# A fused attention and feed-forward layer: the softmax probabilities turned by VectorE blocks and a trip through device memory instead of by TensorE

## The chip, the cores and the metric

One core of a Trainium2 chip runs the whole layer in one launch. The metric is the device time of one execution in microseconds, lower is better. Three runs of the kernel before took 946.12, 946.64 and 946.98 us, median 946.64.

## The reference

A residual stream `x` of 2 batches of 1024 tokens and 512 features passes a gated linear attention, then a feed-forward block, then a softmax attention, then the same feed-forward block again. The part that the change touches is the softmax attention (full, no causal mask, scores over all 1024 tokens of a batch):

```python
scale = 1.0 / jnp.sqrt(jnp.asarray(x.shape[-1], x.dtype))
Q = jnp.einsum('bsd,de->bse', x, W_q)
K = jnp.einsum('bsd,de->bse', x, W_k)
```

then softmax of the scaled Q K^T over the keys, times V, times W_o, added to the stream. The kernel folds W_q with W_k, and W_v with W_o, ahead of time.

## The kernel before, in words

Each engine has an instruction queue of its own, written out by hand; an engine runs its queue strictly in order and waits on semaphores. The stages follow one another: "A" (linear attention, batches 0 and 1), "mid" (weights), "F1" (feed-forward, two blocks), "B" (softmax attention, batches 0 and 1, about 468 to 723 us of the span), "F2" (feed-forward, two blocks). Products are made in f16 or f32r as a high part and a low part, three matmuls for each product (high by high, low by high, high by low).

Stage B, for each batch `b`: tokens are in 8 tiles (rows) of 128. `query` makes the left operands, four for each half of the batch. `values(i)` makes the value tile i. The scores of a pair of rows (rows 2p and 2p+1) come from seven sub-products ("pieces" 1 to 7, a Strassen-like scheme), each six matmuls in one PSUM bank: pieces 1, 6, 7, 4 pass one after the other through bank 4, and pieces 2, 5, 3 through bank 5. ScalarE copies bank 4 to `probs` (`part_sum`), VectorE adds bank 5 to it (`part_add`). Then for row i: VectorE `row_max(i)`, ScalarE `softmax(i)` (exp in place in `probs[i % 2]`, 128 x 1024 f32), TensorE `turn_probs(i)` (eight 128x128 transposes into two PSUM banks), ScalarE `pT_high(i)` (high f16 part of the turned tile), VectorE `pT_low(i)` (low part), TensorE `attend(i)` (24 matmuls), VectorE `out_add(i)` (divide by the row sum, add to the stream).

Between these, the next block's input is normalised and turned (sets B1 or F2): VectorE `x_stats`, `x_normalise`, `x_second`, `x_34_low`; TensorE `turn_both`; ScalarE `x_copy`, `x_row_highs`, `x_12_high`, `x_34_high`; GpSimd `x_sums` and the low parts. `query_parts` on VectorE and GpSimd, with `a_copy`, `a_highs`, `s_high` on ScalarE, split the queries.

There is no planner: the order of work is the order of the calls in each engine's queue. In the stages before and after B, three of the six input sets (F1, B0, F3) are already turned without TensorE: `x_blocks` (VectorE, 32x32 blocks in place), `blocks_to_dram` and `blocks_to_turned` (the SP queue, four transfers out and four back for a 128 x 1024 tile).

```python
def turn_probs(i):
    use = turn_use(b, i)
    pe.wait_ge(probs_done, b * 8 + (i + 1))
    u.free(use)
    ...
    for t in range(BT):
        last = nc.tensor.transpose(bank(use[0], 2)[:, t * P:(t + 1) * P],
                                   probs[i % 2][:, t * P:(t + 1) * P], ident[:, :])
    last.then_inc(filled[use[0]], 1)
```

Of the kernel before, what the change touches and what calls it, by code (L numbers as in the profile page):

```python
# [5 lines left out]
F32 = mybir.dt.float32  # L6
# [39 lines left out]

X_STATS = {(0, 2): ((0,), (1,), (2, 3)), (0, 3): ((4,), (5,), (6, 7))}
# [24 lines left out]
def ffn_uses(**more):  # L72
    uses = {0: 24, 1: 20, 2: 13, 3: 12, 4: 10, 5: 2, 6: 2, 7: 2}
    for name, n in more.items():
# [10 lines left out]
          ("B", 0, {0: 13, 1: 13, 2: 8, 4: 16, 5: 12, 6: 5, 7: 5}),  # L85
          ("B", 1, {0: 10, 1: 10, 2: 7, 4: 17, 5: 12, 6: 4, 7: 4}),
# [28 lines left out]
def hybrid_layer_kernel(nc, x, wq, wk, wv, w_ab, bq, bk, bv, b_ab,  # L115
# [3 lines left out]
    def at(name, offset, cols, dtype=F32):  # L119
# [18 lines left out]
           for v in range(2)]  # L138
# [76 lines left out]
               (Z + 112896, Z + 114944, Z + 116992), (Z + 86016, Z + 88064, Z + 90112))  # L215
# [57 lines left out]
    turned_lo = [at(f"turned_lo{b}", (Z + 47104, Z + 8192)[b], BTOK, F16) for b in range(2)]  # L273

# [5 lines left out]
    blocks = nc.dram_tensor("blocks", [4 * len(MOVED), QUADS, 2 * KT, P, SQ], F32, kind="Internal").ap()  # L280

# [117 lines left out]
    row_a_done = sem("row_a_done")  # L399
    row_b_done = sem("row_b_done")  # L400
# [179 lines left out]
    def pT(b, i):  # L580

        if i < 3:
            return tuple(t[b][:, :].rearrange("p (g n) -> p g n", g=2) for t in (turned_hi, turned_lo))
        if (b, i) in ((1, BT - 1), (1, BT - 2)):
            c = BTOK * (BT - 1 - i)
            return tuple(t[:, c:c + BTOK].rearrange("p (g n) -> p g n", g=2) for t in (s_hi, s_lo))
        return tuple(t[b][:, :].rearrange("p (k n) -> p k n", k=KT)[:, 0:2, GROUP:BTOK] for t in (xb_hi, xb_lo))
# [58 lines left out]
    def score_use(piece, p):  # L646
        return {1: (4, 4 * p), 6: (4, 4 * p + 1), 7: (4, 4 * p + 2), 4: (4, 4 * p + 3),
                2: (5, 3 * p), 5: (5, 3 * p + 1), 3: (5, 3 * p + 2)}[piece]

    def turn_use(b, i):  # L650
        return (4, 16) if (b, i) == (1, BT - 1) else (2, i)
# [24 lines left out]
    with block as blk:  # L676

        @blk.sync
        def _(sp):
# [126 lines left out]

            weights_out()
            for q in MOVED:
# [6 lines left out]
                if q == B0:  # L815
                    weights_back()
            store(0, *range(BT))
# [6 lines left out]
        def _(pool):  # L824
# [221 lines left out]

            query_parts(0, 0)
# [3 lines left out]
            query_parts(1, 0)  # L1051
            x_rstd(F2, *range(8))
            pool.wait_ge(x_34_lo, 4 * B1 + 4)
            for dst, src, less in ((3, 7, 1), (4, 2, 0), (5, 3, 1)):
                nc.gpsimd.tensor_tensor(cols(w_s, dst, HID), cols(w_gu, src, HID), cols(w_s, less, HID),
                                        ALU.subtract).then_inc(ws_ready, 1)
            query_parts(1, 1)
            pairs_of(F2)
            ffn("F2", 0)
# [4 lines left out]
        def _(act):  # L1064
# [335 lines left out]
            for b in range(BATCHES):  # L1400
# [6 lines left out]
                def part_sum(piece, p):  # L1407
# [3 lines left out]
                    row, half = {1: (0, 0), 6: (0, 1), 7: (1, 1), 4: (1, 0)}[piece]  # L1411
                    nc.scalar.activation(cols(probs[row], half), bank(4), ACT.Copy).then_inc(drained[4], 1)  # L1412
# [7 lines left out]
                def pT_high(i):  # L1420
                    use = turn_use(b, i)
                    u.full(use)
                    nc.scalar.activation(pT(b, i)[0], bank(use[0], 2).rearrange("p (g n) -> p g n", g=2), ACT.Copy,  # L1423
                                         scale=PS).then_inc(pT_hi_done, 1)

# [9 lines left out]
                for i in range(1, 6):  # L1435
                    v_high(i)
                part_sum(1, 0)
                part_sum(6, 0)
                part_sum(7, 0)
                v_high(6)  # L1440
                part_sum(4, 0)
                softmax(0)
                v_high(7)
                for p in range(4):
                    if (b, p) == (1, 3):
                        softmax(7)
                    pT_high(2 * p)
                    if p == 1:
                        a_copy(b, 1, 0)
                    elif p < 3:  # L1450
                        part_sum(1, p + 1)
                    if (b, p) != (1, 3):
                        softmax(2 * p + 1)
                    if p == 1:
                        a_copy(b, 1, 1)
                        a_highs(b, 1, 0)
                        s_high(b, 1, 0)
                        a_highs(b, 1, 1)
                        s_high(b, 1, 1)
                    if p == 2:  # L1460
                        x_34_high(B1 if b == 0 else F2, 1)
                    if p == 3 and b == 0:
                        x_34_high(B1, 3)
                        a_copy(1, 0, 0)
                        a_copy(1, 0, 1)
                    if p == 3 and b == 1:
                        x_copy(F2, 3)
                        x_highs(F2, 3)
                    pT_high(2 * p + 1)
                    if p == 1:  # L1470
                        part_sum(1, 2)
                    if p < 3:
                        part_sum(6, p + 1)
                        part_sum(7, p + 1)
                    q = B1 if b == 0 else F2
                    if p in (1, 2):
                        x_copy(q, 2 * p - 2)
                        x_highs(q, 2 * p - 2)
                    if p == 2 and b == 0:
                        x_copy(q, 3)  # L1480
                        x_row_highs(q, 3)
                    if p < 3:
# [1258 lines left out]
```

## Time and profile before

| what | value |
|---|---|
| median of three runs | 946.64 us |
| the profiled execution's own time | 945.55 us |
| its span in the profile | 943.8 us |
| TensorE busy | 930.4 us, 99% |
| VectorE, ScalarE, GpSimd busy | 608.2, 445.3, 425.9 us (64%, 47%, 45%) |
| matmul clock granted | full in all 40 slices |
| DMA in stage B | close to idle |

Engines are named PE (TensorE matmul), PEld (its weight loads), DVE (VectorE), ACT (ScalarE), POOL (GpSimd), SPq (the SP engine's DMA queue). L numbers are lines of the kernel. Matmul ends are modelled, so the start-to-start distance is the cost of a matmul on the engine.

### The profile page before, as it was taken

The page shows a single profiled execution, that of the slowest core. Times are in us where ns is not written, and L with a number is a line of the kernel's source. Part 1 is how long each engine was busy: PE and PEld are TensorE (multiplying, and loading weights), DVE is VectorE, ACT ScalarE, POOL GpSimd, SP SyncE. Part 2 cuts the span into 40 slices and gives each one's busy share as a digit, 9 for nine tenths or more (in the row PEclk, how much of TensorE's full clock was granted, in tenths as well). Part 3 has the DMA queues.
Part 4 walks back from the last instruction along what each step waited for, and adds up shares of the span by engine and source line. Part 5 has one row for each costly group of instructions (what it writes and reads, how often), then busy time and mean ns, then how long its engine had stood idle before and what let it go on. Part 6 is the DMA issues. An engine that isn't in the chain of part 4 may idle for free.

```text
span 943.8 us, 13107 instructions
## 1 busy us (share of the span) xinstructions
PE 930.4 (99%) x4654; PEld 525.6 (56%) x4670; DVE 608.2 (64%) x1148; ACT 445.3 (47%) x884; POOL 425.9 (45%) x447
## 2 busy tenths in 40 slices
PE   7999999999999999999999999999999999999998
PEld 4888988888734444444444455444455444444444
DVE  7555656949777777767655466446466777766643
ACT  4443334356577634663333354323455686246620
POOL 5433424377357654665630043304333466545530
PEclk9999999999999999999999999999999999999999
DMA  9501300024211190015500000000000001910001
GB/s 314 181 11 34 134 23 23 1 91 135 68 66 45 23 157 1 1 23 81 107 14 1 1 1 1 1 1 1 1 1 1 1 1 23 186 59 1 1 34 56
DMA packets 115008, 44.97 MB, mean 48 GB/s; under 512 B 101952, under 2 KB 102272, under 8 KB 114688
## 3 DMA queue, kind: packets, MB, share of 16 engines
q1 hardware_dynamic: 114944, 44.13, 18.1%
q8 instruction: 38, 0.62, 0.3%
q14 instruction: 26, 0.21, 0.1%
HBM read 32.56 MB, written 11.57 MB: 47 GB/s over the span
## 4 chain that ended last, share of the span: by engine, by line
PE 93%; DVE 2%; ACT 1%; POOL 1%; DMA 1%; SPq 1%; issue 1%; DVEq 0%; POOLq 0%
PE psum L2211 54%; PE psum L2458 14%; PE psum L2460 13%; PE psum L2608 7%; PE psum L2619 1%; DMA bq_col<-bq 1%; PE psum L2260 1%; PE psum L2345 1%; PE psum L2249 1%; ACT probs L1417 0%; DVE xb_lo L2116 0%; ACT xb_hi L1423 0%; DVE ln_bn L1532 0%; POOL wvT_lo L1007 0%; SPq L686 0%
## 5 line engine op out<-in xcount | busy, mean ns | idle before, releaser
L972 POOL TENSOR_TENSOR hid<-hid,hid_hi 128x512 f32<-128x512 f32 x88 | 102.9, 1170 | 110.1 <-DVE hid_hi L1888 110.1
L2458 PE MATMUL psum<-xf,w_gu 128*128 128x512 f16 x352 | 133.8, 380 | 0.1
L2458 PE MATMUL psum<-xf,w_s 128*128 128x512 f16 x264 | 100.1, 379 | 1.5 <-DVE up L1861 1.3
L2460 PE MATMUL psum<-xf,w_gu 128*128 128x512 f16 x264 | 100.0, 379 | 0.0
L2211 PE MATMUL psum<-wd_low,hid_lo 128*128 128x512 bf16 (+1 forms) x330 | 73.8, 373 | 0.2
L1286 ACT ACTIVATE hid_lo<-hid 128x512 f16<-128x512 f32 x88 | 54.9, 624 | 33.3 <-POOL hid L972 33.3
L968 POOL TENSOR_TENSOR hid<-up,gate 128x512 f32<-128x512 f32 x44 | 56.1, 1274 | 25.2 <-ACT gate L1281 25.2
L2460 PE MATMUL psum<-xq,w_s 128*128 128x512 f16 x176 | 66.7, 379 | 0.0
L2458 PEld LDWEIGHTS psum<-xf,w_gu 128*128 128x128 f16 x352 | 34.3, 97 | 54.6 <-ACT acc L1271 15.5
L1281 ACT ACTIVATE gate<-gate,sg_xs 128x512 f32<-128x512 f32 x44 | 31.7, 721 | 58.4 <-DVE gate L1871 58.4
L2211 PEld LDWEIGHTS psum<-wd_low,hid_lo 128*128 128x128 f16 x330 | 32.3, 98 | 36.8
L834 POOL TENSOR_TENSOR xrstd<-xvar,minus_half 128x1 f32<-128x1 f32 x48 | 25.5, 551 | 59.2 <-DVE xvar L1536 59.2
L1853 DVE TENSOR_TENSOR gate<-psum,acc 128x512 f32<-128x512 f32 x44 | 30.4, 692 | 31.1 <-ACT acc L1259 23.5
L1888 DVE TENSOR_SCALAR hid_hi<-hid 128x512 f16<-128x512 f32 x88 | 39.1, 444 | 16.1 <-POOL hid L968 14.6
L2211 PE MATMUL psum<-wd_b,hid_hi 128*128 128x512 bf16 (+1 forms) x190 | 45.8, 372 | 0.2
L2458 PEld LDWEIGHTS psum<-xf,w_s 128*128 128x128 f16 x264 | 25.9, 98 | 35.8 <-issue 4.9
L1871 DVE TENSOR_TENSOR gate<-psum,acc 128x512 f32<-128x512 f32 x44 | 30.4, 690 | 20.4 <-PE psum L2460 20.0
L2460 PEld LDWEIGHTS psum<-xf,w_gu 128*128 128x128 f16 x264 | 25.8, 98 | 30.8
L1412 ACT ACTIVATE probs<-psum 128x512 f32<-128x512 f32 x32 | 19.1, 597 | 48.3 <-PE psum L2608 48.3
L1880 DVE SCALAR_TENSOR_TENSOR hid<-psum,su_c,gate 128x512 f32<-128x512 f32 x44 | 33.0, 750 | 12.5 <-PE psum L2460 12.5
L1970 DVE TENSOR_TENSOR yt<-psum,sd_rows 128x512 f32<-128x512 f32 x31 | 21.1, 687 | 28.7 <-PE psum L2211 27.7
L1861 DVE SCALAR_TENSOR_TENSOR up<-psum,su_c,acc 128x512 f32<-128x512 f32 x44 | 33.0, 749 | 9.1 <-POOL hid L968 7.6
(336 smaller groups left out, 2430.8 us busy)
## 6 DMA issues: line engine op xcount, KB each, us to landing
turned<-blocks SPq DMA_DIRECT2D x36, 128.0 KB, 3.0
cla_wide<-cla_dram SPq DMA_DIRECT2D x16, 256.0 KB, 3.3
out<-xres SPq DMA_DIRECT2D x15, 256.0 KB, 2.0
xres<-x SPq DMA_DIRECT2D x3, 1024.0 KB, 13.0
blocks<-xn SPq DMA_DIRECT2D x24, 128.0 KB, 3.1
codes_gu<-gateT SPq DMA_DIRECT2D x1, 2816.0 KB, 11.5
codes_gu<-upT SPq DMA_DIRECT2D x1, 2816.0 KB, 10.6
codes_da<-downT SPq DMA_DIRECT2D x1, 1536.0 KB, 6.7
```

Source lines behind the costliest of these rows:

```text
L968: nc.gpsimd.tensor_tensor(hid2[:, :], up2[:, :], gate2[:, :], ALU.mult).then_inc(hid2_done, 1)
L972: nc.gpsimd.tensor_tensor(hid[:, :], hid[:, :], hid_part(hid_hi, j, half), ALU.subtract).then_inc(rest_done, 1)
L1281: nc.scalar.activation(gate2[:, :], gate2[:, :], ACT.Silu, scale=sg_xs[:, j:j + 1]).then_inc(silu2_done, 1)
L1286: nc.scalar.activation(hid_part(hid_lo, j, half), hid[:, :], ACT.Copy, scale=LO).then_inc(lo_done, 1)
L1853: nc.vector.tensor_tensor(cols(gate1, j % 2), bank(2), acc1[:, :], ALU.add).then_inc(drained[2], 1)
L1861: nc.vector.scalar_tensor_tensor(out=up2[:, :], in0=bank(3 + j % 2), scalar=su_c[:, j:j + 1], in1=acc3[:, :], op0=ALU.mult, op1=ALU.add).t ...
L1880: nc.vector.scalar_tensor_tensor(out=hid1[:, :], in0=bank(j % 2), scalar=su_c[:, j:j + 1], in1=cols(gate1, j % 2), op0=ALU.mult, op1=ALU.m ...
L1888: nc.vector.tensor_scalar(hid_part(hid_hi, j, half), hid[:, :], ROUND, -ROUND, ALU.add, ALU.add).then_inc(hi_done, 1)
L2211: return nc.tensor.matmul(out, lhsT, rhs, start=start, stop=stop)
L2458: nc.tensor.matmul(bank(use[0]), w, x_operand(piece, k, False), start=start and k == 0, stop=False, skip_group_check=not start)
L2460: last = nc.tensor.matmul(bank(use[0]), w, x_operand(piece, k, True), start=False, stop=k == 1, skip_group_check=not start)
L2608: last = nc.tensor.matmul(bank(use[0]), l, r, start=start and k == 0 and j == 0, stop=k == 1 and j == 2, skip_group_check=not start)
```

## The change

Of the 16 rows of probabilities, 15 are turned in a new way (all but row 7 of batch 1). VectorE transposes the 32x32 blocks of `probs[i % 2]` in place (`p_blocks`), SP sends the tile to device memory in four transfers and fetches it back in four with the blocks put in their places (`probs_turned`, into the same buffer), and `pT_high` and `pT_low` read the turned tile in SBUF and not in PSUM. `probs[i % 2]` is free for the next pair only when `pT_low(i)` is done, and ScalarE's `part_sum` waits for that. The last row is still turned by TensorE, in banks 2 and 3.

Piece 5 now has bank 2 and piece 3 bank 3, so pieces 1, 2, 6, 5, 3 run as one group (`first_row`), which completes the even row; pieces 7 and 4 complete the odd one and are put in the middle and behind `attend(2p)`. The first group is put in front of `values(3)`. All queues are reordered to fit; the copies and splits of the next input set (`x_both`, `x_12_high`, `x_34_high`, `x_second`) are at new places. The even rows' turned parts get a buffer `even_hi`, `even_lo` in the place of two weight sums `w_s`, which GpSimd therefore makes after `attend(4)` of batch 1; four weight sums are made, not three.

```diff
+                def p_blocks(i):
+                    dve.wait_ge(probs_done, b * 8 + (i + 1))
+                    nc.vector.transpose(probs[i % 2][:, :], probs[i % 2][:, :]).then_inc(p_blocks_done, 1)
...
+            def probs_turned(b, i):
+                n, t = b * BT + i, probs[i % 2]
+                sp.wait_ge(p_blocks_done, n + 1)
+                src = t[:, :].rearrange("p (m j) -> p m j", j=SQ)
+                for a in range(QUADS):
+                    sp.dma_start(prob_blocks[n, a].rearrange("m (c i) j -> i (m c) j", c=QUADS),
+                                 src[a * SQ:(a + 1) * SQ, :, :]).then_inc(p_out[i % 2], 16)
+                sp.wait_ge(p_out[i % 2], p_all(b, i))
+                dst = t[:, :].rearrange("p (m a j) -> p m a j", a=QUADS, j=SQ)
+                for a in range(QUADS):
+                    sp.dma_start(dst[:, :, a, :],
+                                 prob_blocks[n, a].rearrange("m p j -> p m j")).then_inc(p_moved[i % 2], 16)
...
                 def part_sum(piece, p):
...
+                    if probs_free(b, 2 * p + row) > 0:
+                        act.wait_ge(pT_lo_done, probs_free(b, 2 * p + row))
...
                 def pT_high(i):
-                    use = turn_use(b, i)
-                    u.full(use)
+                    if last_tile(b, i):
+                        u.full(LAST_TURN)
+                    else:
+                        act.wait_ge(p_moved[i % 2], p_all(b, i))
+                    if i > 1:
+                        u.full(out_use(b, i - 2))
```

TensorE's new queue for the pairs (before, each row had a `turn_probs` in front of its `attend`):

```python
for i in range(3): values(i)
first_row(0)                        # pieces 1, 2, 6, 5, 3
for i in range(3, 6): values(i)
score(7, 0); values(6); score(4, 0); values(7)
for p in range(4):
    if p < 3: first_row(p + 1)
    if p == 2: turn_both(2)
    if (b, p) == (1, 3): turn_last(7)
    attend(2 * p, 0, 4)
    if p < 3: score(7, p + 1)
    attend(2 * p, 4, 8)
    if p < 3: score(4, p + 1)
    if p == 0: query(b, 1, 0..3)
    elif p == 1: turn_both(1)
    elif (b, p) == (0, 3): query(1, 0, 0..3)
    attend(2 * p + 1)
    if p == 0: turn_both(0)
    elif p == 2: turn_both(3)
```

ScalarE's new queue, from `part_sum(7, 0)` on: `part_sum(7, 0)`, `part_sum(4, 0)`, `softmax(1)`, `v_high(6)`, `pT_high(0)`, `v_high(7)`, and then for each p < 3: `part_sum(1)`, `part_sum(6)` of pair p+1; p = 1: `x_both(0)`, p = 2: `x_12_high(1)`; `pT_high(2p+1)`; `softmax(2p+2)`; p = 1: `x_12_high(0)`, `x_34_high(0)`, p = 2: `x_34_high(1)`, `x_both(2)`; `part_sum(7)`, `part_sum(4)`, `softmax(2p+3)`; p = 0: `a_copy` twice, `a_highs`, p = 1: `x_both(1)`, p = 2: `x_12_high(2)`; `pT_high(2p+2)`; then the rest.

VectorE's new queue, from `row_max(1)` on: `row_max(1)`, `v_low(6)`, `p_blocks(1)`, `pT_low(0)`, `v_low(7)`, two `x_stats`, and then for each p < 3: `part_add(2)`, `part_add(3)` (two additions), `row_max(2p+2)`, `pT_low(2p+1)`, `p_blocks(2p+2)`; p = 0: four `x_stats`, p = 1: `x_second(0)`, `x_normalise(1)`, p = 2: `x_34_low(1)`; `out_add(2p)`, `part_add(5)`, `row_max(2p+3)`, `p_blocks(2p+3)`, `pT_low(2p+2)`, with further steps of the next input set between them.

## Rows read from the trace of the kernel before

**Rows 1.** The page: busy time, the TensorE clock and the DMA by slice, the chain.

```profile
PE 930.4 (99%) x4654; PEld 525.6 (56%) x4670; DVE 608.2 (64%) x1148; ACT 445.3 (47%) x884; POOL 425.9 (45%) x447
...
PEclk9999999999999999999999999999999999999999
DMA  9501300024211190015500000000000001910001
...
PE 93%; DVE 2%; ACT 1%; POOL 1%; DMA 1%; SPq 1%; issue 1%; DVEq 0%; POOLq 0%
```

**Rows 2.** Busy time of each engine in two stretches, batch 0 and 1 of stage B.

```profile
468.00:609.00 141.00, 140.72 (x698) 69.15 (x697) 80.93 (x143) 58.68 (x94) 40.19 (x42) 1.00 0.02 8
609.00:723.00 114.00, 113.91 (x575) 57.10 (x573) 65.55 (x120) 48.21 (x78) 36.10 (x34) 1.00 0.00 1
```

**Rows 3.** TensorE in order of time: a turned row, a piece's last matmul, the next attend.

```profile
563.21 1.04 PE L2619 MATMUL psum<-ident,probs 128*128 128x128 f32 x8
564.08 0.38 PE L2608 MATMUL psum<-xb_hi,a_hi 128*128 128x512 f16 x1
564.30 0.38 PE L2608 MATMUL psum<-xb_lo,a_hi 128*128 128x512 f16 x1
...
566.46 0.38 PE L2608 MATMUL psum<-xb_hi,a_lo 128*128 128x512 f16 x1
567.12 0.39 PE L2211 MATMUL psum<-v_hi,xb_hi 128*128 128x512 f16 x1 [0.28 <-DVE xb_lo L2116]
```

**Rows 4.** VectorE, ScalarE in order of time: from the last part_add to the exp.

```profile
504.81 0.69 DVE L2098 TENSOR_TENSOR probs<-psum,probs 128x512 f32<-128x512 f32 x1
505.61 1.22 DVE L2108 TENSOR_REDUCE smax<-probs 128x1 f32<-128x1024 f32 x1
506.86 0.21 DVE L2110 TENSOR_SCALAR nmax<-smax,mids 128x1 f32<-128x1 f32 x1
...
507.11 1.24 ACT L1417 ACTIVATE probs<-probs,nmax,mids 128x1024 f32<-128x1024 f32 x1 [0.41 <-DVE nmax L2110]
508.26 0.19 ACT L1417 ACTIVATION_READ_ACCUMULATOR probs<-probs,nmax,mids 128x1 f32 x1
```

**Rows 5.** Groups of stage B by line and shape: busy, mean ns of one.

```profile
L1412 ACT ACTIVATE probs<-psum 128x512 f32<-128x512 f32 x32 | 19.1, 597 | 48.3 <-PE psum L2608 48.3
L1397 ACT ACTIVATE s_hi<-s_f 128x1024 f16<-128x1024 f32 x6 | 6.3, 1057 | 11.7 <-POOL s_f L1027 7.1 <-DVE s_f L2069 4.6
...
L2116 DVE SCALAR_TENSOR_TENSOR xb_lo<-psum,xb_hi 128x1024 f16<-128x1024 f32 x8 | 9.8, 1225 | 8.8 <-ACT xb_hi L1423 8.8
```

**Rows 6.** The instructions on tile xn_pair: VectorE's block transpose of a 128x1024 f32 tile.

```profile
L1559 DVE STREAM_TRANSPOSE xn_pair<-xn_pair x3: 1245/1245/1246, 338.2 to 809.9; 128x1024 f32<-128x1024 f32 x3
```

**Rows 7.** Four transfers out with nothing else in flight (311 to 315 us).

```profile
L763 SPq DMA_DIRECT2D blocks<-xn x4: 343/590/620, 311.7 to 313.3; - x4
...
DMA to landing us min/median/max: 2.1/2.6/4.2
```

**Rows 8.** Four transfers back on SP, and ScalarE's instruction that waited for them.

```profile
345.67 2.80 SPq L782 DMA_DIRECT2D turned<-blocks  x4
...
350.88 0.42 ACT L1092 ACTIVATE xf<-turned 128x256 f16<-128x256 f32 x1 [1.93 <-DMA turned<-blocks]
```

**Rows 9.** VectorE in order of time: from the first of four x_stats to out_add.

```profile
512.83 0.69 DVE L1532 BATCH_NORM_STATS2 ln_bn<-xres 128x6 f32<-128x512 f32 x1
...
516.85 0.20 DVE L2124 TENSOR_SCALAR mids<-rowsum,mids 128x1 f32<-128x1 f32 x1
```

**Rows 10.** VectorE and GpSimd in order of time: x_second's last step, the two sums.

```profile
556.02 0.42 DVE L1580 TENSOR_TENSOR x_mid<-psum,x_mid 128x256 f32<-128x256 f32 x1
...
556.52 0.73 POOL L844 TENSOR_TENSOR x_last<-x_mid,x_first 128x256 f32<-128x256 f32 x1 [7.83 <-DVE x_mid L1580]
557.21 0.90 POOL L846 TENSOR_TENSOR x_last<-x_first,x_mid 128x256 f32<-128x256 f32 x1
```

**Rows 11.** TensorE after its two longest idle times of the span.

```profile
4.07 4.34 PE L2211 MATMUL psum<-mask_b,ident_b 128*128 128x512 bf16 x10 [4.07 <-POOL mask_b L875]
...
18.83 0.50 PE L2211 MATMUL psum<-wv_hi,xt_hi 128*128 128x512 f32 x1 [1.34 <-ACT ab_row L1145]
19.16 0.39 PE L2211 MATMUL psum<-wv_lo,xt_hi 128*128 128x512 f32 x1
19.39 0.40 PE L2211 MATMUL psum<-wv_hi,xt_lo 128*128 128x512 f32 x1
```

More of the change, by code:

```diff
@@ L816, in _ @@
                     weights_back()
+                    for b in range(BATCHES):
+                        for i in range(BT - b):
+                            probs_turned(b, i)
             store(0, *range(BT))
@@ L1438, in _, with x_both @@
                 part_sum(6, 0)
+                v_high(VALUES_FIRST[b])
+                softmax(0)
+                for i in range(VALUES_FIRST[b] + 1, 6):
+                    v_high(i)
                 part_sum(7, 0)
+                part_sum(4, 0)
+                softmax(1)
                 v_high(6)
-                part_sum(4, 0)
-                softmax(0)
+                pT_high(0)
                 v_high(7)
+                q = B1 if b == 0 else F2
+                def x_both(i):
+                    x_copy(q, i)
+                    x_row_highs(q, i)
@@ L1444, in _ @@
                 for p in range(4):
-                    if (b, p) == (1, 3):
-                        softmax(7)
-                    pT_high(2 * p)
+                    if p < 3:
+                        part_sum(1, p + 1)
+                        part_sum(6, p + 1)
                     if p == 1:
[L1449 to L1453, printed above, removed]
@@ L2644, in turn_both, with first_row, turn_last @@
                     turn_x(q, i, 1)
+                def first_row(p):
+                    for piece in (1, 2, 6, 5, 3):
+                        score(piece, p)
+                def turn_last(i):
+                    pe.wait_ge(probs_done, b * 8 + i + 1)
+                    u.free(LAST_TURN)
+                    u.free((3, 4))
+                    for t in range(BT):
+                        last = nc.tensor.transpose(bank(LAST_TURN[0], 2)[:, t * P:(t + 1) * P],
+                                                   probs[i % 2][:, t * P:(t + 1) * P], ident[:, :])
+                    last.then_inc(filled[LAST_TURN[0]], 1)
                 if b == 0:
@@ L2648, in _ @@
                         query(0, 0, n)
-                for i in range(6):
+                for i in range(VALUES_FIRST[b]):
                     values(i)
-                for piece in (1, 2, 6, 5, 7):
-                    score(piece, 0)
+                first_row(0)
+                for i in range(VALUES_FIRST[b], 6):
+                    values(i)
+                score(7, 0)
                 values(6)
-                score(3, 0)
                 score(4, 0)
@@ L2703, in _ @@
+                    elif p == 1:
+                        turn_both(1)
+                    elif (b, p) == (0, 3):
+                        for n in range(4):
+                            query(1, 0, n)
+                    attend(2 * p + 1)
+                    if p == 0:
+                        turn_both(0)
+                    elif p == 2:
+                        turn_both(3)
             ffn("F2", 0)
```

312 lines of the change are left out of this document (153 added, 159 removed).

## The prediction

> **What bounds the kernel now.** I read the page first: TensorE is busy 99% of the span at the full clock, and the chain that ended last is 93% TensorE [rows 1]. Then the busy time by stretch for stage B: in batch 0 TensorE idles 0.28 us of 141, in batch 1 0.09 us of 114, while VectorE works 57% and ScalarE 42% of the time, and DMA does next to nothing [rows 2]. So only two things change the time here: work taken off TensorE, and waits put on it. Then TensorE in order of time. Matmuls start 0.2155 us apart, so a score piece (6) costs 1.29 us, a query, a value tile or half an attend (12) 2.59, an attend 5.17. Eight transposes of a row hold the engine from 563.21 to 564.08, 0.87 us; `turn_both` is eight of the same [rows 3].
>
> **What is removed.** 15 rows x 0.87 = 13.05 us of TensorE work, all of it on the path that sets the end. Of the 0.37 us that TensorE idled in stage B, 0.3 was a wait for the split of a row just turned [rows 3], and goes with it: 13.35.
>
> **What is added, and how long a row takes.** The transposes were 0.87 us of work; the new way is no work for TensorE but a long chain. With S the moment when an even row's last piece (3) is done:
> - TensorE to VectorE 0.2 (a modelled matmul of 0.38 less the 0.2155 to the next, and 0.03 of hand-over [rows 3]); two additions, 0.8 each to the next dependent step; reduce to negated maximum to exp 505.61 to 507.11 = 1.5 [rows 4]. Exp starts at S + 3.3.
> - exp and its accumulator 507.11 to 508.45, and 0.03 on: `p_blocks` starts at S + 4.67 [rows 4] and takes 1.245 [rows 6]: S + 5.92.
> - Trip out: the four issues start within 1.6 us, and with nothing else in flight a transfer lands in 2.6 (median) [rows 7]: 4.3. Trip back: 345.67 to 350.88 = 5.2, with outgoing transfers about [rows 8]. With hand-over I take 9.5 for both. Bounds: 8.4 (2 x 4.2, both alone), 11.2 (both 5.2, and 0.8 for longer landings, as the 4.2 maximum shows [rows 7]). The transfers are of exactly this shape, so this is close. SP is held 4.3 + 2.8 = 7.1 us by a row, under the 10 us between rows, so SP itself is no bound.
> - `pT_high` from SBUF 1.06, `pT_low` 1.23 [rows 5]: the row is ready at S + 17.85.
>
> In front of a row's attend, TensorE has other work; the question is whether it is enough, and what is queued behind the rows on ScalarE and VectorE, because TensorE's pieces 1, 6, 7, 4 share bank 4 and each waits until ScalarE has copied the last one (0.6 [rows 5]). I walked the three queues of a batch in the order written, and found the stalls below. Moved steps that I find in TensorE's shadow cost nothing: `turn_both`, whose `x_normalise` comes 1 us or more ahead; the late weight sums (GpSimd is idle two thirds of stage B [rows 2]; piece 7 of F2 needs them some 5 us after they end); SP's other transfers of stage F2, which come later anyway.
>
> **Stall 1, `part_sum(1)` of pair 1.** It writes `probs[0]`, so it waits for `pT_low(0)`. Count from the end of pair 0's piece 4. Copy 0.8, then reduce to exp 1.5: exp at 2.34; `v_high(6)` 3.6 to 4.2; `v_low(6)` from 4.25; `p_blocks(1)` 4.86 to 6.1; `pT_low(0)` to 7.23; copy; TensorE may start piece 6 at 7.93. It is there at 5.17 (`values(7)`, pieces 1 and 2). Stall 2.76. The trip of row 0 was over before, so this does not hang on it.
>
> **Stalls 2 and 3, row 1 and the queries.** Same origin. Row 1 is back at 6.1 + 9.5 = 15.64. `pT_high(1)` stands in front of `softmax(2)`, and `part_sum(7)` waits for `pT_low(1)` at 18.03: bank 4 is free for piece 4 at 18.75, and TensorE is there at 5.17 + 2.76 + 3.88 + 6.47 = 18.3. Stall 0.45. `softmax(2)` is done at 18.0, `p_blocks(2)` at 19.3, and behind it VectorE has four `x_stats`, 512.83 to 516.85 = 4.02 [rows 9], `out_add(0)` 1.1, `part_add(5)` 0.7, and the maximum and exp of row 3 (0.1 + 1.5 + 1.3); only then ScalarE copies the first query out of bank 0 (0.6): 28.6. The third query needs that bank; TensorE is there at 18.75 + 1.29 + 5.17 = 25.2. Stall 3.4.
>
> **Stall 4, pair 2.** ScalarE has `x_12_high(0)` and `x_34_high(0)` in front of `part_sum(7)`. They wait for `x_second(0)`, which VectorE has behind `p_blocks(4)`: S + 5.85, two steps to S + 6.7, GpSimd's sums 556.44 to 558.11 = 1.67 [rows 10], S + 8.4; `x_34_high` and the copy, S + 9.6. TensorE wants bank 4 for piece 4 at S + 6.47 (attend 5.17, piece 7 1.29). Stall 3.15. No trip is in it.
>
> **Stall 5, pair 3.** 0.05, the same place with less in front.
>
> **Stall 6, `attend(6)`.** There is no pair 4 to fill the time: from S TensorE has `turn_both(2)`, attend, two pieces, attend, `turn_both(3)` = 0.87 + 5.17 + 2.59 + 5.17 + 0.87 = 14.67, against the row's 17.85. Stall 3.2; in batch 1 the last row's turn (0.87) fills part: 2.3.
>
> Sum: batch 0 2.76 + 0.45 + 3.4 + 3.15 + 0.05 + 3.2 = 13.0; batch 1 12.1; 25.1 in all, less 13.35: **+11.8 us**. The profiled execution took 945.55 with a span of 943.8, so its like would be 957.3 with a span of 955.6; the median of the runs is 1.09 above it: 946.64 + 11.8 = **958.4**. With the trips at 8.4 the stalls are 2.76 + 0 + 2.6 + 3.15 + 0 + 2.1 in a batch, 20.4 in all: 953.7. With 11.2, 2.76 + 2.15 + 3.4 + 3.15 + 1.3 + 4.9, 34.5 in all: 967.8.
>
> The rows show a 128 KB transfer landing in 2.6 to 3.1 us [rows 7, 8]. The Trainium skill, DMA: Bandwidth & Descriptors, "Anatomy of one DMA", fits 2.0 us plus the bytes at 436 GB/s, an estimate of 2.3 us here, though for the GpSimd path; trips of 7.9 in all would give about 952. The rows' figure is used. What a row costs where it is turned is 0.87 us on TensorE against 1.24 on VectorE and 9.5 in transfers [rows 3, 6 to 8]. The Trainium skill, VectorE: DVE Perf Modes, "Rules for kernel authors", would have a 128x128 transpose on TensorE where PSUM will do; going by that rule no time is won by the move, while going by TensorE's busy share alone 13 us are.
>
> **The rivals.**
> 1. *VectorE's side work does not stand in the way (faster).* Place: VectorE's queue between a row's maximum and the block transpose. Stalls 1, 3 and 4 exist only because `v_low(6)`, four `x_stats` with `out_add`, and `p_blocks(4)` with `x_second(0)` come ahead of what ScalarE waits for. If these were done early enough, stall 1 is 1.9, 3 and 4 are 0, and a batch stalls 5.6 and 4.7: 10.3 - 13.35 = -3.0, 943.6. It decides once all stalls together are under 11.4 us. For it: VectorE idles 43% of the stage. Against it: each queue is in order, and `p_blocks` itself waits for the exp.
> 2. *All waits are hidden (faster).* The 13.35 is kept whole: 933.3. For it: the 19 us between a row's scores and its attend, in most pairs, exceed 17.85. Against it: bank 4 and `probs` are wanted long before the attend.
> 3. *No effect.* Stalls of 11.4 to 15.2 us; no one mechanism gives it, it lies between.
> 4. *The clock falls too (much slower).* TensorE was granted its upper level in all slices [rows 1], and a wait of 1.34 us left its matmuls 0.23 us apart. But the ten matmuls after the first 4.07 us without work took 4.34 us, 0.434 each, half speed, though the clock column says full: 2.2 us lost [rows 11]. Seven of the new waits are 2.7 to 3.4 us, between those two. If each drew that loss, and the eighth (2.3), 8 x 2.2 = 17.6: 976. The Trainium skill, TensorE: Matmul & The Clock Gate, its advice against idle gaps over some 3 us between bursts, speaks for it; by that rule the time would be up to this 976, and the trace shows only that 4.07 does and 1.34 does not.
>
> **How the numbers follow.** The forecast (the walk, trips 8.4 to 11.2, 953.7 to 967.8) has 0.70; shorter trips or a stall mis-sized, 949 to 953.7, 0.08; rival 4 0.07; rival 1 0.08; rival 2 0.03; rival 3 0.04. The range 950 to 970 leaves out the two faster cases, no effect and the upper half of rival 4: under 2 in 10. Faster by over 0.2% (1.9 us, about what a measurement tells from no change) 0.11, within it 0.04, slower 0.85.
>
> **What would show it.** In the profile after: TensorE busy in stage B down by 13 us and idle up by 25; `part_sum` (now with a VectorE releaser) as the releaser of the score pieces, `a_copy` of the third query, and `pT_low` of the first matmul of `attend(6)`; VectorE with 15 more transposes of 1.24 us; the trip from `p_blocks` to `pT_high` 9.5 us. The prediction is wrong if the score pieces never wait, if the third query starts at once, or if the trips take under 7 us.

## The result, and the profile after

Four runs of the changed kernel took 963.81, 965.72, 960.68 and 960.99 us, median 962.40, where the kernel before took 946.44 (946.12 to 946.98) beside them. The ratio is 1.0172, 95% interval 1.0141 to 1.0204: slower by 16 us. The profiled execution has a span of 962.1 us, against 943.8. (One of the four runs of e1_x34_later below took 1942.74 us, twice the others, and is left out of its median and ratio.)

The page of the kernel after: busy time, the TensorE clock and the DMA by slice, the chain, the DMA issues.

```profile
PE 925.9 (96%) x4550; PEld 514.9 (54%) x4550; DVE 633.0 (66%) x1171; ACT 444.2 (46%) x884; POOL 430.8 (45%) x448
...
PEclk9999999999999999999999989999999999999999
DMA  9401300034301370018215445115452001920001
...
PE 79%; DVE 7%; SPq 3%; DMA 3%; ACT 2%; POOL 2%; issue 2%; DVEq 0%; ACTq 0%; POOLq 0%
...
prob_blocks<-probs SPq DMA_DIRECT2D x60, 128.0 KB, 2.7
probs<-prob_blocks SPq DMA_DIRECT2D x60, 128.0 KB, 3.1
```

Against [rows 1] TensorE's busy time fell by 4.5 us only, not by 13, although 120 transposes are gone (the weight loads, PEld, fell from 4670 to 4550; the matmul count before has 16 fewer records than weight loads); its idle time (span less busy) rose from 13.4 to 36.2 us. So two things happened: waits of 22.8 us came, and the work that is left took 8.5 us longer than it should have (13.05 less 4.5). The clock row has one slice below the top.

Every first matmul of TensorE in stage B that had waited 0.2 us or more, in order of time (batch 0 to 600 us, then batch 1):

```profile
515.12 0.38 PE L2681 MATMUL psum<-xs_hi,s_hi 128*128 128x512 f16 x1 [2.62 <-ACT probs L1459]
...
535.78 0.38 PE L2284 MATMUL psum<-xb_hi,g_hi 128*128 128x512 f16 x1 [1.98 <-ACT a_f L1424]
...
564.73 0.58 PE L2681 MATMUL psum<-xs_hi,a_hi 128*128 128x512 f16 x1 [2.92 <-ACT probs L1459]
...
600.45 0.39 PE L2284 MATMUL psum<-v_hi,even_hi 128*128 128x512 f16 x1 [4.12 <-DVE even_lo L2179]
...
658.02 0.38 PE L2681 MATMUL psum<-xs_hi,s_hi 128*128 128x512 f16 x1 [2.62 <-ACT probs L1459]
...
668.91 0.38 PE L2681 MATMUL psum<-xs_hi,a_hi 128*128 128x512 f16 x1 [0.37 <-ACT probs L1459]
...
678.58 0.38 PE L2284 MATMUL psum<-xb_hi,g_hi 128*128 128x512 f16 x1 [3.03 <-ACT a_f L1424]
...
705.84 0.38 PE L2681 MATMUL psum<-xs_hi,a_hi 128*128 128x512 f16 x1 [2.92 <-ACT probs L1459]
...
737.09 0.39 PE L2284 MATMUL psum<-v_hi,s_hi 128*128 128x512 f16 x1 [1.70 <-DVE s_lo L2179]
```

L2681 is a score piece, L2284 the third query or the first matmul of `attend(6)`; L1459 is `part_sum`, L1424 `a_copy`, L2179 `pT_low`. The nine waits sum to 22.3 us. In order, they are at the places of stalls 1, 3, 4, 6 (batch 0) and 1, 2, 3, 4, 6 (batch 1) of the prediction's walk through the queues, with the releasers that it named. (A tenth, 1.09 us at 364.92, is in F1, where the kernel before had none; it comes before the changed stage, and the same place had 0.37 in e4, 0.79 in e2, 0.74 in e10 and under 0.2 in e3, so it varies from run to run or version to version; its cause is open.)

The first of them, read on the two engines that cause it. ScalarE and VectorE of the kernel after:

```profile
511.21 1.04 ACT L1474 ACTIVATE even_hi<-probs 128x1024 f16<-128x1024 f32 x1
512.15 0.58 ACT L1450 ACTIVATE v_hi<-psum 128x512 f16<-128x512 f32 x1
514.38 0.60 ACT L1459 ACTIVATE probs<-psum 128x512 f32<-128x512 f32 x1 [1.64 <-DVE even_lo L2179]
```

```profile
511.34 0.69 DVE L2138 SCALAR_TENSOR_TENSOR v_lo<-psum,v_hi 128x512 f16<-128x512 f32 x1 [1.88 <-ACT v_hi L1450]
511.95 1.23 DVE L2175 STREAM_TRANSPOSE probs<-probs 128x1024 f32<-128x1024 f32 x1
513.11 1.18 DVE L2179 SCALAR_TENSOR_TENSOR even_lo<-probs,even_hi 128x1024 f16<-128x1024 f32 x1
```

VectorE makes the value tile's low part and the block transpose of row 1 before it comes to `even_lo`, the last reader of `probs[0]`; ScalarE waits for that 1.64 us with bank 4 full, and TensorE waits for bank 4. VectorE itself was idle 1.88 us just before.

The trip of row 1 of batch 1, first SP's queue, then ScalarE's `pT_high`:

```profile
656.11 2.25 SPq L836 DMA_DIRECT2D prob_blocks<-probs  x4
660.48 2.86 SPq L841 DMA_DIRECT2D probs<-prob_blocks  x4
```

```profile
665.76 1.06 ACT L1474 ACTIVATE turned_hi<-probs 128x1024 f16<-128x1024 f32 x1 [5.65 <-DMA probs<-prob_blocks]
```

From the first issue out to the first issue back it is 4.37 us, from there to `pT_high` 5.28, 9.65 in all. Seven of the 15 rows have a `pT_high` that waited for its transfers; there the trip took 9.08 to 10.75 us, the longest in row 6 of batch 0: out 587.33 to 592.92, `pT_high` at 598.08.

The granted clock, in stretches of 1 us after the first wait of batch 0 and after the first of batch 1 (the column third from the right):

```profile
515.00:516.00 1.00, 0.88 (x5) 0.43 (x6) 0.93 (x4) 0.00 (x0) 0.03 (x1) 1.00 1.24 200
516.00:517.00 1.00, 1.00 (x4) 0.39 (x3) 0.93 (x4) 0.03 (x1) 0.53 (x2) 0.54 0.98 151
517.00:518.00 1.00, 1.00 (x3) 0.30 (x2) 0.51 (x1) 0.57 (x1) 0.52 (x1) 0.50 0.00 0
518.00:519.00 1.00, 1.00 (x4) 0.44 (x3) 0.00 (x0) 0.00 (x0) 0.00 (x0) 0.50 0.26 43
519.00:520.00 1.00, 1.00 (x5) 0.36 (x4) 0.00 (x0) 0.00 (x0) 0.00 (x0) 0.75 1.13 178
...
658.00:659.00 1.00, 0.98 (x5) 0.51 (x6) 0.93 (x4) 0.00 (x0) 0.13 (x1) 1.00 1.23 199
659.00:660.00 1.00, 1.00 (x7) 0.42 (x5) 0.93 (x4) 0.49 (x1) 0.53 (x2) 1.00 0.84 130
660.00:661.00 1.00, 1.00 (x6) 0.45 (x5) 0.42 (x1) 0.11 (x1) 0.42 (x1) 1.00 0.00 0
```

About 1 us after the end of the same wait of 2.62 us, TensorE was granted its lower level (1.2 GHz) for some 3.4 us in batch 0 and kept the upper one (2.4 GHz) in batch 1. In the whole of this execution the clock fell at 516.1, 536.4, 563.9 (for 6.8 us) and 601.4, all in batch 0, and not once in batch 1. The mean of 0.991 over 962.1 us is 17.3 us at half speed, 8.7 us of work lost (8.5 by stretches of 1 us, of which 0.4 fell into the wait before 564.73, where nothing was lost).

The account of the span: 943.8 - 13.35 saved + 22.3 waits + 1.1 in F1 + 8.7 clock = 962.6, against 962.1.

### The profile page after: what moved, and what is told of

Its sections match the earlier page's. It is cut to its first block, busy times and chain, and to the rows that moved or that the text cites. A ratio compares the mean times of both kernels' runs of the same rounds, so it can differ in the third digit from the quotient of the medians.

```text
span 962.1 us, 13054 instructions
## 1 busy us (share of the span) xinstructions
PE 925.9 (96%) x4550; PEld 514.9 (54%) x4550; DVE 633.0 (66%) x1171; ACT 444.2 (46%) x884; POOL 430.8 (45%) x448
## 4 chain that ended last, share of the span: by engine, by line
PE 79%; DVE 7%; SPq 3%; DMA 3%; ACT 2%; POOL 2%; issue 2%; DVEq 0%; ACTq 0%; POOLq 0%
PE psum L2284 45%; PE psum L2531 14%; PE psum L2533 13%; PE psum L2681 6%; DVE smax L2168 1%; DMA probs<-prob_blocks 1%; DMA bq_col<-bq 1%; DMA prob_blocks<-probs 1%; SPq L786 1%; PE psum L2333 1%; SPq L805 1%; ACT probs L1464 1%; DVE probs L2175 1%; PE psum L2418 1%; DVE ln_bn L1588 1%
## 5 line engine op out<-in xcount | busy, mean ns | idle before, releaser
L2284 PE MATMUL psum<-wd_low,hid_lo 128*128 128x512 bf16 (+1 forms) x330 | 73.8, 373 | 0.0
L2284 PEld LDWEIGHTS psum<-wd_low,hid_lo 128*128 128x128 f16 x330 | 32.3, 98 | 36.8
L2284 PE MATMUL psum<-wd_b,hid_hi 128*128 128x512 bf16 (+1 forms) x198 | 48.1, 373 | 0.0
L1459 ACT ACTIVATE probs<-psum 128x512 f32<-128x512 f32 x32 | 19.0, 595 | 49.3 <-PE psum L2681 44.5
L2284 PE MATMUL psum<-wd_a,hid_hi 128*128 128x512 bf16 (+1 forms) x165 | 39.9, 373 | 0.0
```

The source lines that it names most:

```text
L2284: return nc.tensor.matmul(out, lhsT, rhs, start=start, stop=stop)
```

## The experiments

All ratios are to the kernel before, run beside each; "waits" is the sum of TensorE's waits of 0.2 us or more in stage B, and "clock" the mean granted clock, both of the profiled execution.

| kernel | rows on the trip | waits, us | clock | median, us | ratio (95%) |
|---|---|---|---|---|---|
| after | 15 | 22.3 | 0.991 | 962.40 | 1.0172 (1.0141 to 1.0204) |
| e1_x34_later | 15 | 19.9 | 0.991 | 960.90 | 1.0160 (1.0143 to 1.0177) |
| e2_stats_later | 15 | 17.0 | 0.996 | 953.38 | 1.0090 (1.0067 to 1.0114) |
| e5_values_first | 15 | 21.6 | 0.993 | 957.89 | 1.0129 (1.0097 to 1.0160) |
| e3_no_trip | none | 16.6 | 0.991 | 956.52 | 1.0113 (1.0098 to 1.0128) |
| e4_filled | 15 | 4.3 + 19.0 filled | 1.000 | 956.04 | 1.0106 (1.0089 to 1.0123) |
| e6_row6_tensor | 13 | 17.7 | 0.994 | 956.52 | 1.0120 (1.0102 to 1.0139) |
| e7_13_rows_order | 13 | 10.8 | 0.998 | 945.54 | 0.9995 (0.9986 to 1.0004) |
| e8_rows46_tensor | 11 | 5.7 | 1.000 | 942.24 | 0.9976 (0.9955 to 0.9998) |
| e9_queries_fill | 11 | 5.8 | 1.000 | 941.98 | 0.9962 (0.9947 to 0.9977) |
| e10_lows_behind | 11 | 1.1 | 1.000 | 937.13 | 0.9905 (0.9891 to 0.9920) |

### e1: the splits of the next set behind `part_sum(7)` and `part_sum(4)`

```diff
@@ ScalarE, each pair
-                    if p == 1:
-                        x_12_high(q, 0)
-                        x_34_high(q, 0)
-                    elif p == 2:
+                    if p == 2:
                         x_34_high(q, 1)
...
                         part_sum(4, p + 1)
+                        if p == 1:
+                            x_12_high(q, 0)
+                            x_34_high(q, 0)
                         softmax(2 * p + 3)
```

> The changed kernel, with x_12_high(0) and x_34_high(0) taken from in front of part_sum(7) of pair 2 and put behind part_sum(4) on ScalarE. Theory A (the stalls are one chain, each moved along when one is taken away): the two waits of 2.92 us before piece 4 of pair 2 go, but row 4 is ready only 18.4 us after its last piece while TensorE, now 2.9 us earlier, wants bank 4 for piece 6 of pair 3 at 16.4: a new wait of about 2.7 us stands there, and the time moves by under 1 us apart from the clock. Theory B (the stalls add up, each is worth its own length): both waits go and nothing takes their place, 5.8 us faster than the changed kernel, near 956 us, and a half-clock stretch of 7 us less in batch 0.

Measured: TensorE's waits between 560 and 580 us of e1.

```profile
563.61 0.66 PE L2333 MATMUL psum<-ident,xn 128*128 128x128 f32 x4 [0.21 <-DVE xn L1598]
...
574.31 0.38 PE L2681 MATMUL psum<-xs_hi,s_hi 128*128 128x512 f16 x1 [2.27 <-ACT probs L1459]
```

Stall 4 (2.92 us) is gone from both batches, so its cause is shown. Theory A held: a wait of 2.27 and 2.05 us (batch 0 and 1) stands before piece 6 of pair 3, where there was none: `part_sum(1)` of pair 3 waits for row 4, whose trip was behind stall 4 before. The waits shrank by 2.4 us net; the median of the three runs is 1.5 us lower, less than the spread of the changed kernel's runs. Mending one order uncovers the next length of the chain.

### e2: four `x_stats` behind `p_blocks(3)`

```diff
@@ VectorE, each pair
-                    if p == 0:
-                        for l in range(4, 8):
-                            x_stats(q, l)
-                    elif p == 1:
+                    if p == 1:
                         x_second(q, 0)
...
                         p_blocks(2 * p + 3)
                     if p == 0:
+                        for l in range(4, 8):
+                            x_stats(q, l)
                         query_parts(b, 1, 0)
```

> The changed kernel, with the four x_stats of VectorE moved from behind p_blocks(2) to behind p_blocks(3). Theory A: these 4.02 us are what holds the copy of the first query; the wait before the third query (1.98 and 3.03 us) goes to 0 in both batches and no new one comes, since pair 2 has no such tight distance: 5 us faster than the changed kernel, 957 us or less with the clock. Rival (the trip of rows 1 and 2 holds the queries): the wait stays above 2 us.

Both query waits (1.98 and 3.03) are gone and none came in their place; the others stayed at 2.62, 2.93, 3.84 and 2.62, 0.34, 2.92, 1.72. The span fell by 10.6 us: 5.3 of waits, and some 4.9 because the clock was 0.996 and not 0.991 (3.8 us of work lost and not 8.7); so half of the gain is the clock, and one of the four runs, at 0.991, took 958.04. It is the largest gain of a single edit that leaves all 15 rows on the trip, for four steps moved on an engine that is idle a third of the time.

### e5: the value tile 6 split ahead of row 1's maximum

```diff
@@ ScalarE, and likewise VectorE with v_low(6) ahead of row_max(1)
                 part_sum(7, 0)
+                v_high(6)
                 part_sum(4, 0)
                 softmax(1)
-                v_high(6)
                 pT_high(0)
```

> The changed kernel with v_high(6) in front of part_sum(4) and softmax(1) on ScalarE, and v_low(6) in front of row_max(1) on VectorE. Theory A: the wait before piece 6 of pair 1 (2.62 us in both batches) is made of the queue in front of pT_low(0): by the rows it shrinks by 1.1 us, to 1.5; the trip of row 1 starts 1.15 us earlier and so its wait stays as it is. About 2.2 us faster than the changed kernel, apart from the clock. Rival: the trip of row 0 holds it; then it stays at 2.6.

TensorE in batch 0 of e5, and the same 1.54 in batch 1:

```profile
514.22 0.38 PE L2681 MATMUL psum<-xs_hi,s_hi 128*128 128x512 f16 x1 [1.54 <-ACT probs L1459]
```

Stall 1 went from 2.62 to 1.54 in both batches, as expected, so 1.08 of it is `v_low(6)` in the way; what makes the 1.54 that stay is open. Part of it moved on, which was not expected: stall 2 went from 0.37 to 0.99 in batch 1. The waits before the third query are 3.04 in both batches, for a reason of the clock (below, stall 3). In all the waits are only 0.7 us shorter, and the four runs lie between 954.52 and 961.55 with clocks of 0.998 to 0.993: the 4.5 us of the median cannot be put down to the edit.

### e3: no trip

```diff
-                            probs_turned(b, i)
...
-                        act.wait_ge(p_moved[i % 2], p_all(b, i))
+                        act.wait_ge(p_blocks_done, b * BT + i + 1)
```

> The changed kernel without the 120 transfers: SP sends and fetches nothing, pT_high waits for the block transpose alone. The blocks are not put in their places, so the attended values are of other columns. Theory A (queue order makes more than half of the waits): the waits of 2.6 before piece 6 of pair 1, 2.3 to 3 before the third query and 2.9 before piece 4 of pair 2 stay in both batches, those before attend(6) (4.1 and 1.7) and before piece 4 of pair 1 (0.4) go: 15 to 17 us idle are left of 22, near 955 us with some clock loss. Rival (the trip makes the waits): all go, the time is near 933 to 936, faster than before.

Without the transfers the blocks stay where they are, so e3 gives the time of the queues and not the layer's output. TensorE's waits of e3 in batch 0:

```profile
513.31 0.58 PE L2678 MATMUL psum<-xs_hi,s_hi 128*128 128x512 f16 x1 [2.62 <-ACT probs L1456]
...
533.95 0.38 PE L2281 MATMUL psum<-xb_hi,g_hi 128*128 128x512 f16 x1 [1.99 <-ACT a_f L1421]
...
561.22 0.59 PE L2678 MATMUL psum<-xs_hi,a_hi 128*128 128x512 f16 x1 [2.93 <-ACT probs L1456]
...
592.84 0.39 PE L2281 MATMUL psum<-v_hi,even_hi 128*128 128x512 f16 x1 [1.34 <-DVE even_lo L2176]
```

With a trip of 9 to 11 us taken off every row, 16.6 of the 22.3 us of waits are still there, stalls 1 and 4 within 0.01 us. What hung on the trip is most of the wait before `attend(6)` (4.12 to 1.34 and 1.70 to 0.20) and stall 2 (0.37 to under 0.2), 4.7 us together; the other 1.0 of the difference is the third query of batch 1, 3.03 to 1.99, where the clock fell in e3 and not in the changed kernel. The median is 5.9 us lower, and the kernel is still slower than before by 1.1%. So the transfers make about a third of the 16 us; the larger part is the order of the queues.

### e4: the waits filled with matmuls

```diff
@@ TensorE
+                        if (piece, p) == (6, 1):
+                            fill(10, (3, 1))
                         score(piece, p)
...
+                    if p == 1:
+                        fill(12, (3, 3))
                     if p < 3:
                         score(4, p + 1)
...
+                            if n == 2:
+                                fill(12, (3, 2))
                             query(b, 1, n)
...
+                    if p == 3:
+                        fill(13 if b == 0 else 7, (3, 4))
                     attend(2 * p, 0, 4)
```

(`fill(n, ...)` issues n matmuls of 128x512 into bank 3, whose result nobody reads.)

> The changed kernel with 7 to 13 more matmuls of 128x512 in f16 put in each of the four large gaps of each batch, into bank 3, whose result nothing reads: as much work as the gap is long. Theory (the half clock after gaps costs 5 to 12 us a run on top of the waits): the granted clock is 1.00 throughout, the span is near 953.4 (962.1 less the 8.7 us that a mean clock of 0.991 stands for), the device time near 955, and the runs are within 1 us of each other. Rival (the low clock costs nothing, since TensorE would wait anyway): time stays at 961 to 964 and the gaps after it grow by what the clock gives back.

88 more matmuls (19.0 us) and the kernel is 6.4 us faster than the changed one. The clock row of its page:

```profile
PEclk9999999999999999999999999999999999999999
```

The granted clock is 1.000 in all four runs, and they agree within 0.74 us where those of the changed kernel spread over 5. So the clock's fall costs about 6.4 us in the median, net of the waits that it shortens (waits and filling together are 23.3 us here, against 22.3), and the spread goes with it. What is left is the waits themselves: 943.8 - 13.35 + 19.0 + 4.3 = 953.8 us of span, 954.6 measured; 0.37 of the rest is the wait in F1.

### e6: row 6 turned by TensorE

```diff
@@ TensorE (row 6 in banks 2 and 3; pT_high(6) ahead of softmax(7), pT_low(6) ahead of p_blocks(7))
-                    attend(2 * p + 1)
+                    attend(2 * p + 1, 0, 4)
+                    if p == 2:
+                        turn_last(6)
+                    attend(2 * p + 1, 4, 8)
```

> The changed kernel with row 6 of both batches turned by TensorE (eight transposes in banks 2 and 3 in the middle of attend(5)); 13 rows still make the trip. Theory A: the waits before attend(6) (4.12 and 1.70 us) go, for 2 x 0.87 us of TensorE work: 4.1 us faster than the changed kernel, apart from the clock. Rival: another step holds attend(6) as well (pT_high(6), pT_low(6) in their queues), and 1 us or more of the wait stays.

The waits before `attend(6)`, 4.12 and 1.70 us, are gone for 0.87 us of transposes each, as theory A had it. In batch 0 a wait of 1.63 us came at the third query of batch 1, whose bank ScalarE copies behind `pT_high(7)`.

### e7 and e8: the edits together, and row 4 as well

e7 is e1, e2, e5 and e6 in one kernel (13 rows on the trip). e8 also has row 4 turned by TensorE, in banks 2 and 3 within `attend(3)` (diff against e7):

```diff
-    TURNS = {(0, 6): (2, 4), (1, 6): (2, 4), (1, 7): (4, 16)}
+    TURNS = {(0, 4): (2, 3), (1, 4): (2, 3), (0, 6): (2, 5), (1, 6): (2, 5), (1, 7): (4, 16)}
...
-                    attend(2 * p + 1, 0, 4)
-                    if p == 2:
-                        turn_last(6)
-                    attend(2 * p + 1, 4, 8)
+                    ahead = 6 if p == 1 else 4
+                    attend(2 * p + 1, 0, ahead)
+                    if p in (1, 2):
+                        turn_last(2 * p + 2)
+                    attend(2 * p + 1, ahead, 8)
```

> e1, e2, e5 and e6 together, and row 4 of both batches turned by TensorE in the middle of attend(3), since e1 showed its trip to be the next wait behind the one taken away; 11 rows still make the trip. Theory A: from 955.2 without the clock's loss, less 5 (queries), 5.8 - 1.7 (row 4), 4.1 (row 6), 2.2 (values): 940 us, faster than the kernel before by 6, at full clock nearly throughout since no gap is over 1.6 us. Theory B (once trips are in the loop, TensorE waits as much elsewhere): not under 946.

> Change against the changed kernel (962.4 us): the reorderings of e1_x34_later, e2_stats_later and e5_values_first together, and row 6 of each batch turned by TensorE as in e6_row6_tensor; 13 rows make the trip and row 4 is one of them. It tells how much of what e8 gained came from the order of steps and how much from taking row 4 off the trip. Theory A (the order makes most waits; row 4 on the trip costs one of 2.1 us in a batch, as in e1): waits left 1.54 + 0.2 + 2.27 + 0.2 + 1.6 in batch 0 and 1.54 + 1 + 2.05 + 0.2 in batch 1, 10.6 in all, against 11.3 + 0.3 saved: 1.0 us faster than before, near 945.5, if no wait draws a fall of the clock. Rival B (taking row 4 off changed nothing but its own 1.74 us): the waits are those of e8 (5.0 less the 0.72 that hung on row 4), and the time is 1.7 us below e8, 940.5.

e8 measured 942.24 us, 2 above its expectation and the first version that is faster than the kernel before, if barely (its interval reaches 0.9998). e7 measured 945.54, the 945.5 of its theory A. Its waits in all, 10.8 us, are as expected too (10.6); that the median agrees to a tenth is partly luck, since that figure supposed no fall of the clock, and eight of the twelve runs have one (0.996 to 0.999). Its waits in the second half of batch 0:

```profile
566.30 0.38 PE L2688 MATMUL psum<-xs_hi,s_hi 128*128 128x512 f16 x1 [2.26 <-ACT probs L1463]
...
597.89 0.38 PE L2291 MATMUL psum<-xb_hi,g_hi 128*128 128x512 f16 x1 [1.62 <-ACT a_f L1423]
```

Row 4 on the trip costs the 2.26 and 2.05 us before piece 6 of pair 3, and saves 0.87 in each batch. The order alone, with those 13 rows, brings the kernel back to where it was before the change. What goes beyond that is to take the rows off the trip that have too little TensorE work in front of their attend. In the profiles that step is 5.2 us of waits less for 1.7 us of transposes, and the median is 3.3 us lower; the intervals of the two ratios overlap (0.9955 to 0.9998 and 0.9986 to 1.0004), so its size is known less well than its direction in the traces.

### e9: two queries put where TensorE waits

```diff
@@ TensorE (ScalarE's a_copy put forward likewise, query_parts together, x_stats behind)
                     for piece in (1, 2, 6, 5, 3):
+                        if (piece, p) == (6, 1):
+                            query(b, 1, 0)
                         score(piece, p)
...
+                    if p == 0:
+                        query(b, 1, 1)
                     if p < 3:
                         score(4, p + 1)
```

> e8 with the first query of the second half put in front of piece 6 of pair 1 and the second in front of piece 4, where TensorE waits for the block transposes' rows, their copies put forward on ScalarE, the two query_parts put together and the four x_stats behind them. Theory A: the last waits (1.5 and 0.4 us in each batch) are filled with work that is there anyway: 3 to 4 us faster than e8, near 936.5. Rival: the second half's operands (s_lo on GpSimd) come too late for piece 6 of pair 2, since two queries fewer stand in front of it, and a wait of 1 to 3 us takes the place.

The 1.54 us waits went, and 1.71 us waits came before piece 1 of pair 2, so that e9 is no faster than e8 (941.98 against 942.24, where theory A had 936.5). The rival was right that the operands come too late, but named `s_lo` and piece 6; it was `a_lo` and piece 1. GpSimd of e9, where the last row is the one waited for:

```profile
532.50 0.67 POOL L1071 TENSOR_TENSOR a_lo<-a_f,a_hi 128x256 f16<-128x256 f32 x1 [16.57 <-ACT a_hi L1436]
536.57 3.14 POOL L1073 TENSOR_TENSOR s_lo<-s_f,s_hi 128x1024 f16<-128x1024 f32 x1 [3.40 <-ACT s_hi L1443]
539.66 0.72 POOL L1066 TENSOR_TENSOR s_f<-a_f 128x256 f32<-128x256 f32 x1
540.34 0.67 POOL L1071 TENSOR_TENSOR a_lo<-a_f,a_hi 128x256 f16<-128x256 f32 x1
```

Again an engine that had been idle (3.40 us) does the long step first and the short one, which is wanted, behind it.

### e10: GpSimd's two `s_lo` behind both `a_lo`, one `a_copy` forward

```diff
@@ GpSimd, query_parts
-                    pool.wait_ge(s_hi_done, n + 1)
-                    nc.gpsimd.tensor_tensor(s_cols(s_lo, c), sf[:, :].rearrange("p (i n) -> p i n", i=4),
-                                            s_cols(s_hi, c), ALU.subtract).then_inc(s_lo_done, 1)
+                    if s == 0:
+                        low(c)
+                if s == 1:
+                    low(0)
+                    low(1)
@@ ScalarE
                         x_both(3)
+                        if b == 0:
+                            a_copy(1, 0, 0)
                     pT_high(2 * p + 1)
```

> Change against e9_queries_fill (941.98 us): in the split of the second half's queries GpSimd makes both s_f and a_lo first and both s_lo behind them, and ScalarE copies the first query of batch 1 (a_copy) in front of pT_high(7) of batch 0. 11 rows still make the trip. Theory A (the waits left over are an order of steps on one engine, not a lack of time): GpSimd's a_lo, which was ready at 540.9 behind 3.14 us of s_lo, is ready at some 537, before TensorE is through with attend(1) and turn_both(0) at 539.4, so the two waits of 1.71 before piece 1 of pair 2 go; the wait of 1.47 before the third query of batch 1 goes as well, since its bank is copied at 593.5 and not behind pT_high(7). 4.9 us less: span about 935.4, median about 937.1. Rival B (the wait only moves on, as in e1_x34_later): s_lo of the second column half, now the last, is late by 1 us or more for a later piece of pair 2 in both batches: 939 to 940. Rival C: nothing changes, 942.

Measured 937.13 us (936.91 to 937.17), span 935.4. Theory A held. All of TensorE's waits of 0.2 us or more in stage B of e10, and its page:

```profile
575.86 0.38 PE L2710 MATMUL psum<-xs_hi,a_hi 128*128 128x512 f16 x1 [0.57 <-ACT probs L1475]
...
701.32 0.38 PE L2710 MATMUL psum<-xs_hi,a_hi 128*128 128x512 f16 x1 [0.57 <-ACT probs L1475]
```

```profile
PE 920.2 (98%) x4566; PEld 515.9 (55%) x4582; DVE 628.9 (67%) x1167; ACT 443.8 (47%) x884; POOL 431.0 (46%) x448
...
PEclk9999999999999999999999999999999999999999
```

The account closes: 11 rows x 0.87 + 0.3 = 9.9 saved, 1.1 of waits back, 8.8 expected, 943.8 - 935.4 = 8.4 measured. TensorE's busy time is 10.2 us under that of [rows 1].

## Why the prediction was right, and where it was off

**The direction and the mechanism were right.** Forecast 958.4, range 950 to 970; measured 962.4. The premise that only TensorE's work and its waits count gives the span within 0.5 us once the clock, which the forecast had at nothing, is counted (account above). That 962.4 came so near to 958.4 is partly luck: the stalls were put 2.8 us too high and the clock's 6.4 were left out.

**What is removed**, 13.35 us: right. It cannot be read off the changed kernel's busy time (4.5 us less), but e10, where the clock held, has 10.2 us less for 11 rows and 0.87 x 11 = 9.6.

**Stall 1** (2.76 walked, 2.62 measured in both batches), **stall 4** (3.15, 2.92 in both), **stall 2** (0.45; 0.37 in batch 1, under 0.2 in batch 0, where the clock had just been low): right, with the releasers named. e5 shows 1.08 of the first and e1 all of the fourth; e3 shows that no trip is in stalls 1 and 4.

**Stall 3**: walked 3.4, measured 3.03 in batch 1 and 1.98 in batch 0. e2 shows the cause, the `x_stats`. The two values have a reason that the walk lacked: TensorE reached the third query later where its clock had fallen before. Over the kernels with the same queues there, the wait is 3.03 or 3.04 where the clock held after the first wait of the batch and 1.98 to 2.00 where it fell (e1 both, e5 neither, e6 batch 1 only, the changed kernel batch 0 only). So a fall there costs 1.7 us of work, and 1.05 of that comes back as a shorter wait.

**Stall 5** (0.05): none seen.

**Stall 6**: walked 3.2 and 2.3, measured 4.12 and 1.70. The trip of row 6 took 10.75 us in batch 0, inside the bounds of 8.4 to 11.2, and not the 9.5 taken. Most of this wait hangs on the trip (e3, where 1.34 and 0.20 stay without it), and all of it goes when TensorE turns the row (e6).

**The sum of the stalls** was 25.1, measured 22.3: 2.8 too much, of which stall 3 makes 1.8.

**The trip**: 9.5 forecast, 9.65 in row 1 of batch 1 and 9.08 to 10.75 in the seven rows that waited for it; right. (The row's ready time of S + 17.85 is 0.14 more than its terms add up to, 17.71, which changes nothing.) The landings of 2.7 out and 3.1 back (page) are above the estimate of 2.3 from the Trainium skill, DMA: Bandwidth & Descriptors, "Anatomy of one DMA", whose fit is for the GpSimd path; the measurement decides.

**The clock was the term that was off.** The sum had it at nothing and gave rival 4 a chance of 0.07. The clock did fall, and cost 8.7 us of work in the profiled execution and about 6.4 in the median (e4). Without it the forecast would have been 2.4 us above the measured time (956.04 in e4), with it it is 4.0 below. Rival 4 itself is too dear, 976: not each wait draws a fall, and a fall costs 1.7, not 2.2. Its ground was one row, a wait of 4.07 at the start of the span [rows 11], and 1.34 as the one that draws none; that row is TensorE's first work of all, and the falls in stage B came after waits of 1.98 to 4.30, most of them below 4.07.

**The rivals 1 to 3.** Rival 1 put its condition at stalls under 11.4 us, reached by mending VectorE's order. Its mechanism is real (e1, e2, e5). Its price is not shown: it left out the waits of 2.27 and 2.05 us before piece 6 of pair 3 that come up once stall 4 is gone (e1). e7, with the orders mended and two rows fewer on the trip, has 10.8 us and only stands even with the kernel before. With all 15 rows on the trip no run has all the orders mended; from e7's 10.8, e1's 4.3 and 1.6 before `attend(6)`, less the 1.6 that turning row 6 on TensorE brought (e6), it would be an estimated 15 us of waits, above the 11.4. Rival 2 is where e10 nearly is: all waits hidden, but for 11 rows. For 15 rows no run reached it: row 4 (e1, e7) and row 6 (e3, e6) have too little work in front of them in every order that was run. Rival 3 wanted stalls of 11.4 to 15.2 us; 22.3 came.

## What to carry to other kernels

When work is moved off the engine that bounds a kernel onto a long chain through others, walk every in-order queue on that chain and ask what stands ahead of each step that frees a buffer: here a few statistics and splits, on engines that are idle a third of the time and more, left 16.6 of the 22.3 us of waits in place when the transfers were taken away. Move those first; then put back on the fast engine just those pieces that have too little work in front of them (4 of 15 rows here; with the orders mended, +16 us became -9). Where a wait cannot be removed, look at the granted clock after it, in stretches of 1 us, before the wait is priced at its own length.

## What the runs showed of the hardware

- TensorE's granted clock fell to its lower level for some 3.4 us at a time (once 6.8), beginning between 0.9 us before and 1.1 us after the end of a wait, at waits from 1.98 us on (e1, 675.53) and up to 4.30 (e1, 597.35). Waits of such lengths also drew none: 2.62 at 658.02, 3.03 at 678.58 and 2.92 at 705.84 in the changed kernel, 2.93 at 558.86 in e2, 2.26 in e7, whose only fall came after 2.05. The length of the wait alone does not decide. In e4, e9 and e10, with no wait over 1.71 us in stage B, the clock was 1.000 in every run; in e8, with none over 1.54 in the profiled one, it was 0.998 in one run of five.

TensorE's wait of 2.05 us in e7, and the stretch of 1 us behind it:

```profile
697.53 0.38 PE L2688 MATMUL psum<-xs_hi,s_hi 128*128 128x512 f16 x1 [2.05 <-ACT probs L1463]
```

```profile
698.00:699.00 1.00, 1.00 (x5) 0.40 (x4) 1.00 (x2) 0.00 (x0) 1.00 (x2) 0.74 0.06 9
```

- The Trainium skill, TensorE: Matmul & The Clock Gate, "Why this matters for your kernels", advises against idle gaps of over some 3 us between bursts. The rows above have falls after waits of 2.0 us as well, and none after one of 3.03: that advice would have left the waits of e7, and all of e1's but the one of 4.30, free of cost, and both kernels had falls at such waits. What else decides is open.
- The block transpose of a 128x1024 f32 tile in place took 1.23 to 1.25 us each of 15 times on `probs`, as on `xn_pair` [rows 6].
